# Token tiles transposed on TensorE, two steps ahead, instead of by DMA, in the expert loop of a gated cross-attention layer

## The reference, cut to what matters

```python
x = x + tanh(g_xattn) * xattn(layernorm(x), ctx, ...)         # 2048 tokens, D = 256
# the feed-forward part, F = 1024, 8 experts, top 2
gate_logits = einsum("bsh,eh->bse", x, gate_w)                # x: layernorm of the line above
top_v, top_i = top_k(softmax(gate_logits), 2)
for e in range(8):
    h = silu(einsum("bsh,hf->bsf", x, w1[e]) + b1[e])
    y = einsum("bsf,fh->bsh", h, w2[e]) + b2[e]
    out = out + y * comb_w[..., e:e + 1]
x = x + tanh(g_ffn) * out
```

## Time and profile before

| | us |
|---|---|
| median of 3 runs | 350.47 |
| lowest, highest | 349.19, 350.86 |
| the profiled execution's own time | 349.19 |
| its span | 347.5 |
| expert loop on TensorE (first up product to last down product) | 125.0 to 333.4 |
| mean granted TensorE clock | 0.98 of full |

### The profile page before, as it was taken

One profiled execution on the slowest core, in us unless ns is written; L12 is line 12 of the kernel. 1 busy time (PEld: TensorE's weight loads), 2 busy tenths in 40 slices (PEclk: granted clock), 3 DMA queues, 4 the chain that ended last, 5 costly groups with the idle time before them and its releaser, 6 DMA issues.

```text
span 347.5 us, 11173 instructions
## 1 busy us (share of the span) xinstructions
PE 316.7 (91%) x3342; PEld 258.0 (74%) x3342; DVE 259.5 (75%) x593; ACT 174.2 (50%) x490; POOL 198.0 (57%) x227
## 2 busy tenths in 40 slices
PE   7798899999998879999999999999999998999930
PEld 7467788888887767788787887878878786778710
DVE  5769999999998867878788787887878865556620
ACT  2452356565466357656566565665656633253400
POOL 3486889986773142555474655656566463662330
PEclk9999999999999989999999999999999999999985
DMA  7799999998999534354534444445453534353210
GB/s 249 226 375 412 403 420 404 411 408 348 335 380 377 177 80 64 64 63 79 92 59 85 65 79 82 64 90 64 80 78 64 93 52 78 62 84 55 34 21 12
DMA packets 51004, 57.93 MB, mean 167 GB/s; under 512 B 24434, under 2 KB 45154, under 8 KB 48900
## 3 DMA queue, kind: packets, MB, share of 16 engines
q0 software_dynamic: 9408, 26.63, 30.1%
q1 hardware_dynamic: 36212, 27.18, 25.9%
q10 hardware_dynamic: 5328, 3.37, 3.1%
HBM read 42.29 MB, written 10.17 MB: 151 GB/s over the span
## 4 chain that ended last, share of the span: by engine, by line
PE 55%; DVE 23%; DMA 10%; issue 5%; POOL 2%; ACT 2%; POOLq 0%; ACTq 0%; DVEq 0%
PE ps L1151 25%; PE ps L1165 13%; PE ps L1168 7%; DMA out<-sel 6%; DVE ps L1330 5%; DVE sel L1326 3%; DVE w_parts L1326 2%; PE ps L1173 2%; DMA sel<-near_rows,win_near 2%; DVE xs L1362 1%; DVE sel L1601 1%; DVE xn L1598 1%; PE ps L987 1%; DVE ps L1334 1%; DMA near_rows<-w_parts 1%
## 5 line engine op out<-in xcount | busy, mean ns | idle before, releaser
L1151 PEld LDWEIGHTS ps<-sel,w_parts 128*128 x1776 | 121.4, 99 | 34.0 <-issue 6.2
L1151 PE MATMUL ps<-sel,w_parts 128*128 128x128 f16 x1776 | 142.4, 221 | 2.7 <-DVE sel L1601 1.1
L879 ACT ACTIVATE sel<-ps,b1T 128x128 f32<-128x128 f32 x296 | 84.6, 370 | 85.8 <-PE ps L1151 84.0
L644 POOL DMA_INDIRECT out<-sel x37 | 64.7, 1748 | 87.2 <-DVE sel L1601 74.5
L1165 PE MATMUL ps<-w_parts,sel 128*128 x259 | 96.4, 380 | 0.4 <-DVE sel L1567 0.2
L1168 PE MATMUL ps<-w_parts,sel 128*128 x259 | 70.6, 273 | 0.0
L1565 DVE TENSOR_SCALAR sel<-sel 128x512 f16<-128x512 f32 x74 | 32.2, 435 | 28.2 <-ACT sel L879 27.5
L1567 DVE SCALAR_TENSOR_TENSOR sel<-sel 128x512 f16<-128x512 f32 x74 | 51.3, 693 | 2.5
L636 POOL DMA_INDIRECT sel<-tokens_split,sel x37 | 40.4, 1092 | 16.2 <-DVE sel L1535 9.3
L1553 DVE SCALAR_TENSOR_TENSOR w_parts<-w_parts (+1 forms) x32 | 39.0, 1225 | 12.9 <-ACT w_parts L858 11.0
L858 ACT ACTIVATE w_parts<-w_parts (+1 forms) x32 | 34.0, 1067 | 7.0 <-issue 4.4
(11 more groups left out here) (229 smaller groups left out, 422.3 us busy)
## 6 DMA issues: line engine op xcount, KB each, us to landing
w_parts<-in_L_ffn_w SPq DMA_DIRECT2D x16, 1024.0 KB
out<-xs SPq DMA_DIRECT2D x16, 128.0 KB
tokens_split<-xsplit ACTq DMA_DIRECT2D x13, 128.0 KB, 5.7
xs<-in_x ACTq DMA_DIRECT2D x2, 512.0 KB, 7.4
xs<-in_x SPq DMA_DIRECT2D x2, 512.0 KB, 7.3
near_rows<-w_parts SPq DMA_DIRECT2D x4, 256.0 KB, 9.5
sel<-tokens_split,sel POOLq DMA_INDIRECT x37, 3.1
out<-sel POOLq DMA_INDIRECT x37
```

The costliest lines, as they stand in the source:

```text
L644: pool.indirect_dma_start(out_rows, bass.IndirectOffsetOnAxis(slot_row[:, at(q - 1)], 0), y_sb[(k + 3) % 4], None, compute_op=ALU.add).the ...
L879: act.activation(h32[n][:, c * P:c * P + P], ps_h[n][:, c * P:c * P + P], ACT.Silu, bias=biases[:, c:c + 1], scale=1.0 / (X_SCALE * W_SCALE))\
L1151: mm = pe.matmul(ps_h[n][:, c * P:c * P + P], w, xx, start=(i == 0), stop=(i == len(products) - 1))
```

## The change

The DMA transposes and their semaphores go, with SP's part in the loop. TensorE transposes every tile: `turn(q + 2)` stands in step q behind chunk 2 (`TURN_AT = 2`), or, from q = 31 on, between the down and the up products under a branch of its own. It writes PSUM bank 0. DVE copies the result to `xT` with a new instruction at the head of its step (behind `rows_out` from q = 31 on); ACT still copies tile 0. TensorE waits for DVE's copy with `xT_ok` where it waited for the DMA, and its wait on `y_ok` goes. POOL's `slot_w` waits for the transposes on TensorE (`xT_ps`).

```diff
-            def tokens_turned(q):
-
-                with filled(sp, tiles, q):
-                    sp.wait_ge(s[f"gathered{q % 4}"], 16 * (q // 4 + 1))
-                    wait(sp, "h_ps", q * 2 - 2)
-                    sp.dma_start(xT[q % 2], xg16[q % 4], transpose=True).then_inc(s[f"xT_in{q % 2}"], 16)
-
-            for q in range(1, NT):
-                tokens_turned(q)
...
-                        turned(pool, q + 1)
+                        pool.wait_ge(s["xT_ps"], q + 2)
...
-            def first_tokens():
-
-                pe.wait_ge(s["gathered0"], 16)
+            def turn(q):
+
+                pe.wait_ge(s[f"gathered{q % 4}"], 16 * (q // 4 + 1))
                 for h in range(4):
-                    mm = pe.transpose(ps_x16[:, h * P:h * P + P], xg16[0][:, h * P:h * P + P], ident16[:, :])
+                    mm = pe.transpose(ps_x16[:, h * P:h * P + P], xg16[q % 4][:, h * P:h * P + P], ident16[:, :])
                 mm.then_inc(s["xT_ps"], 1)
...
                         pe.wait_ge(s["hlo_ok"], q * 2)
-                        wait(pe, "y_ok", q - 2)
                         for c in range(FC):
                             down_chunk(q - 1, n, c, first, down)
+                    if live(2):
+                        with filled(pe, tiles, q + 2):
+                            pe.wait_ge(s["xT_ok"], q + 2)
+                            turn(q + 2)
...
-                        turned(pe, q + 1)
+                        pe.wait_ge(s["xT_ok"], q + 2)
...
-                        wait(pe, "y_ok", q - 2)
                     for c in range(FC):
...
                             down_chunk(q - 1, n, c, down_first, down)
+                        if live(2) and c == TURN_AT:
+                            with filled(pe, tiles, q + 2):
+                                turn(q + 2)
...
+                if live(2) and 0 < q + 2 and q + 1 < FULL:
+                    tokens_in_place(q, n)
...
+            def tokens_in_place(q, n):
+
+                with filled(dve, tiles, q + 2):
+                    dve.wait_ge(s["xT_ps"], q + 3)
+                    wait(dve, "h_ps", q * 2 + 2)
+                    v.tensor_copy(xT[n].rearrange("p a c -> p (a c)"), ps_x16[:, 0:512]).then_inc(s["xT_ok"], 1)
...
+TURN_AT = 2
```

More of the change, by code:

```diff
@@ L282, in flamingo_layer @@
             rt shifts_ok rt_exp comb_ok rt_ps b2_zeroed row_ps row_ok pad_hot_ok pad_ps pad_ok span_ps span_ok from_ps from_ok prev_ok tables list_ps tile_ps tile_ok prev_ps comb_in
-            slot_w_ok gathered0 gathered1 gathered2 gathered3 xT_ps xT_ok xT_in0 xT_in1 h_ps silu_ok hhi_ok hlo_ok y_half y_ps y_low_ok y_ok scattered out_done""".split()
+            slot_w_ok gathered0 gathered1 gathered2 gathered3 xT_ps xT_ok h_ps silu_ok hhi_ok hlo_ok y_half y_ps y_low_ok y_ok scattered out_done""".split()
         s = {n: sem(n) for n in names}
@@ L335, in filled @@
             return eng.If(tiles > q) if q >= FULL else nullcontext()
[L337 to L342, removed]
         def at(v):
@@ L457, in _ @@
             sp.dma_start(b2_rows[0:2, :], b2_split.rearrange("i e n -> i (e n)")).then_inc(s["b2_rows_in"], 16)
-            sp.wait_ge(s["rt"], RT_LIST)
-            tiles = tile_count(sp)
-            def tokens_turned(q):
-                with filled(sp, tiles, q):
-                    sp.wait_ge(s[f"gathered{q % 4}"], 16 * (q // 4 + 1))
-                    wait(sp, "h_ps", q * 2 - 2)
-                    sp.dma_start(xT[q % 2], xg16[q % 4], transpose=True).then_inc(s[f"xT_in{q % 2}"], 16)
-            for q in range(1, NT):
-                tokens_turned(q)
             for n in range(3):
@@ L474, in _ @@
             sp.wait_ge(s["out_in"], 16 * T)
+            sp.wait_ge(s["rt"], RT_LIST)
+            tiles = tile_count(sp)
             wait(sp, "scattered", tiles * 16)
@@ L1204, in moe @@
                     first_place.append(block_byte(before_of[0], E))
-                    first_tokens()
                 if q == 0:
```

## The result

| us | before | after |
|---|---|---|
| median (8 runs each, same chip) | 350.24 | 354.42 |
| lowest, highest | 349.19, 351.15 | 352.42, 355.64 |
| the profiled execution, its span | 349.19, 347.5 | 353.07, 351.2 |

The ratio of the times is 1.0121, with a 95% interval of 1.0095 to 1.0149.

What follows compares the result with a forecast made beforehand. TensorE was taken as the bound, without slack inside a step. Transposes +8.1, branches +0.5, DMA wait -0.3 and `y_ok` -0.2 gave +8.1 us on the 350.47 median: 358.6 us, range 355.5 to 361.5 for 8 in 10.

Steps and rivals of the forecast that it cites:

- The step, 0.22 us longer: TensorE's loop step: four transposes a tile at 0.055 to 0.060 us each add 0.22 to 0.24, giving 5.61 us.
- Rival 3: Transposes don't overlap in the loop; each holds TensorE for 219 ns, giving 381 us; chance 3%.
- So the gaps are TensorE's own register loads (nine places, the change keeps all): Ahead of some steps' first up matmul: loads, not DMA transposes or `y_ok`, cause about 5.1 us of gaps, which stay.
- all of it lies on the path: On TensorE: nothing in a step waits, so the added transposes cost their full +8.1 us, up to 8.8.
- Rival 4: Not slower: DMA transposes slow TensorE's operand streams and end its gaps; without them 348.0 us; chance 3%.
- rival 1: The gaps on TensorE were the DMA's and go with its transposes, giving 354.0 us; chance 7%.
- Branches, +0.5: From step 31 on, the transposes' own branch costs 0 to 0.2 in each of 6 steps: +0.5 us (0 to 1.2).
- -0.3 for the DMA wait: At the loop's start: TensorE's wait for tile 2's DMA transpose, ending at 133.04, goes: -0.3 us (0 to -0.9).
- +0.44 for half clock: Tile 1's transposes, inside the first up product at half clock, take 0.44 us.
- `y_ok`, -0.2: At the large gap near 287 us, removing TensorE's `y_ok` wait saves 0.2 us (0 to -0.2).
- DVE's copy, 0.69: DVE's new 512-column copy from PSUM takes 0.69 us a tile, by an f32 row, at cost 0 to the whole.
- rival 2: DVE becomes the bound if copy and wait cost 1.6 us, TensorE waiting for L1588: 365 us; chance 5%.

Runs made afterwards that it cites:

- experiment 7: Kernel of experiment 6 with four registers in place of three in the register loads behind step 28: 349.51 us, ratio 0.9986 to the kernel before.
- experiment 11: Kernel of experiment 9 with DVE's `rows_out` ahead of the halves and TensorE's waits on `y_ok` and `w_lo_ok` removed: 344.89 us against 349.19, ratio 0.9887.
- Experiment 1: Kernel before plus four spare 128-column matmuls where the change has its transposes, DMA transposes and waits kept: 354.27 us against 349.08, ratio 1.0144.
- experiment 6: Kernel before with a third `xT` buffer, so each DMA transpose is issued one step earlier: 349.82 us against 350.04, ratio 1.0000.
- second profiles: Both kernels run and profiled once more, unchanged: before 350.05 us, after 354.42 us.
- experiment 3: Changed kernel with TensorE transposing only one of four blocks of each tile from 1 on: 347.58 us against 349.08, ratio 0.9944 to the kernel before.
- experiment 12: Kernel before plus one spare 128-column matmul behind chunk 2 of steps 0 to 30: 349.01 us against 349.19, ratio 0.9997.
- experiment 9: Kernel before with one register load of eight registers in place of two of four: 347.71 us against 349.68, ratio 0.9941.

## Why the prediction was half right

- **The step, 0.22 us longer: right.** Spacing 55 ns, no idle time, no switching cost, no mark of the wait on the gather. Rival 3 is out: the Trainium skill's 390 and 275 ns (VectorE: DVE Perf Modes, The three transpose paths; TensorE: Matmul & The Clock Gate, Part 4) hold here for no transpose as a cost; four of them cost 220 ns.
- **"So the gaps are TensorE's own register loads (nine places, the change keeps all)": the step that failed**, and with it "all of it lies on the path". The cause of the gaps was right, and experiments 7 and 11 show it. The prediction named its own sign of being wrong, that the gap at the register loads goes, and it came (at step 29 in part). But a gap is not the load's time, it is what the queue's lead doesn't cover, and I treated it as fixed while the array's step around it grew. Experiment 1 shows that the growth alone takes the gaps away, 2.9 us. The prediction's own rows would have told. It has loads of 1.54 us at a gap of 1.26. And at 231.0 it sets one load of 0.33 beside the 0.35 by which the step is longer, but two stand there; the second, in the kernel before, is

```profile
L1198 PEldq TENSOR_LOAD <-sel x1: 447/447/447, 231.3 to 231.3; - x1
```

  That is 0.78 us of loads at 0.35 of gap: more than half was already hidden by something, and the prediction didn't ask by what.
- **Rival 4 and rival 1** had the gaps gone too, but through the DMA. By experiments 1 and 6 it wasn't the DMA; rival 1's 354.0 is near the measured time for a wrong reason.
- **Branches, +0.5: too much.** Distances 29 to 36 grew by 1.20 (1.35 in the second profiles), and the six of them with transposes account for 6 x 0.22 = 1.32. The new branch costs nothing that stands out behind four transposes.
- **The start, -0.3 for the DMA wait and +0.44 for half clock: neither as a term.** The wait for tile 2's transpose at 133.04 was a misreading: its row says "issue", 0.18, and the changed kernel has the same row without any DMA transpose:

```profile
132.32 0.69 PE L1134 MATMUL ps<-sel,w_parts 128*128 128x128 f16 x6 [0.18 <-issue]
```

  In the second profile of before TensorE did wait 0.65 us for tile 1's DMA transpose, and that wait is gone. But steps -1 and 0 are the queue's: at half clock the first 48 matmuls took 4.48 us, at full clock in the second profile 4.01, with the transposes in them 4.05 in the changed kernel (124.26 to 128.31). What half clock cost there the next 48 gave back, 3.52 us: both first profiles have 8.06 for the two steps. The half clock of 126 us wasn't there in the profile of after. From first up product to first bias the changed kernel took 8.87 in both its profiles and before 8.87 and 9.57: 0 to -0.7 where my terms gave +0.36.
- **`y_ok`, -0.2, at step 29: fell out larger**, -0.44 there (-0.67 in the second profiles), through the lead again and not through the end of a wait: experiment 1, which keeps `y_ok`, has 6.62 there and the change 6.60.
- **DVE's copy, 0.69: too much, and without consequence.** It is 0.42, and TensorE doesn't wait for it. DVE's groups after, 160 to 280 us:

```profile
L1588 DVE COPY sel<-ps 128x512 f16<-128x512 f16 x21 | 8.9, 424 | 15.2 <-PE ps L1162 8.9 <-issue 6.2
L1596 DVE TENSOR_SCALAR xn<-ps,sel 128x256 f32<-128x256 f32 x22 | 10.5, 478 | 0.0
```

I took the f32 row; this one is f16. The Trainium skill (VectorE: DVE Perf Modes, Why PSUM operands drop a tier) lets a 16-bit PSUM source keep one of the faster modes and gives f32 none; 424 against 693 ns agrees. DVE is idle ahead of the copy for 0.7 us a tile, and TensorE never waits for it, so rival 2 is out. `rows_out` has no idle time ahead of it: as forecast it follows the halves and not TensorE.

Three slips changed nothing: the 0.39 in the bound for the waiting transpose is 0.37 by the earlier trace rows; the gather is issued not three steps but some 7 to 9 us ahead of the transposes in the changed kernel, which was enough; and for the 7.2 at the foot of the range no working is given.

**The sum as it came out:** 7.5 for 34 tiles, -2.45 and -0.44 for the gaps, -0.12 for the end, 0 to -0.7 for the start: 3.8 to 4.5, against 4.2 in the medians.

**What stays open.** The lead isn't won evenly (0.4, then 0.1 and 0.1 in before), so its balance gives sums and not single gaps; why a load of four takes 0.33 at one place and 0.45 at another, and why the loads of step 29 take 0.77 to 1.09, was not found. Whether the removal of the DMA transposes is worth anything in the change itself can't be told: experiment 1, which keeps them, and the change overlap in their intervals. At the shorter step of experiments 3 and 12 something that was removed is worth 1 to 2 us, but it may be the wait.

## What to carry to other kernels

An engine that is busy for all of a stretch can have two paces, its array's and its queue's. Before adding work to it, or taking some away, ask of each instruction on which of the two it lands. In this kernel matmuls without new addresses were free wherever the queue was behind, and waits or register loads, which no busy time counts, cost where it was. A gap shorter than the thing that causes it says that a reserve hides the rest, and a change to the reserve changes the gap.

## What the runs showed of the hardware that I had not expected

- A load of three registers took 770 to 1090 ns, one of four 330 to 450 in three cases of four and up to 880 in the others, one of eight 590 to 910.
- A wait instruction at the head of a step held TensorE's queue for 51 ns; with fewer waits there, six of the seven gaps of 0.2 to 0.4 us at the loads were gone (experiments 9 and 11).
- One spare 128-column matmul in each of 31 steps was free: 349.01 against 349.19.
- Half clock in the first 3 us of the loop cost little, 4.48 against 4.01 us for 48 matmuls, since the queue needs 4.0 anyway, and the next 48 took 3.52 in place of 4.07.
